# A third of an attention tile's probabilities turned by VectorE and a trip through DRAM instead of TensorE, in a three-layer Perceiver kernel

## The reference, cut to what matters

```python
def attention(q, k, v, mask):          # 32 heads of 32, 8 groups that share keys and values
    scores = einsum('bsgrd,btgd->bgrst', q, k) / sqrt(32) + mask
    probs = softmax(scores)            # over the 257 context rows
    return einsum('bgrst,btgd->bsgrd', probs, v)
x = x + attention(layernorm(x), ctx, ctx, mask)
x = x + state_space(layernorm(x))      # a causal convolution with one kernel of 1024 taps, plus D*u
x = x + experts(layernorm(x))          # 64 rank-8 experts, the top 16 of each row weighted by a softmax
```

## Time and profile before

| | |
|---|---|
| median of 3 runs | 1291.4 us (1287.3 to 1295.49) |
| the profiled execution, its own time | 1286.13 us |
| its span from the first to the last instruction | 1284.3 us |
| busy | TensorE 96%, ScalarE 87%, VectorE 76%, GpSimd 64% |
| mean granted TensorE clock | 0.993 of full speed |

### The profile page before, as it was taken

The page is one execution under the profiler, slowest core; times in us unless marked ns, Lnnn a source line. Parts: engine busy times, 40 slices in busy tenths (PEclk is TensorE's granted clock), DMA queues, the critical chain, the costliest instruction groups (busy, mean ns, idle before and its releaser), DMA issues.

```text
span 1284.3 us, 41514 instructions
## 1 busy us (share of the span) xinstructions
PE 1238.2 (96%) x13676; PEld 1075.3 (84%) x13676; DVE 976.1 (76%) x3424; ACT 1121.2 (87%) x3337; POOL 827.1 (64%) x1259
## 2 busy tenths in 40 slices
PE   4679999999999999999999999999999999999997
PEld 3568888888888888888888888888888888888886
DVE  7877777877777777777877877778777777777753
ACT  6999999999899989898998989999998999899851
POOL 5477667677666667766767766676776666677420
PEclk9799999999999999999999999999999999999999
DMA  7543444444443444444344444444444434444210
GB/s 246 158 148 114 139 120 137 139 130 139 130 139 109 148 138 123 130 146 125 117 139 155 122 122 147 117 133 139 137 138 123 139 118 139 138 124 127 55 60 33
DMA packets 150103, 166.38 MB, mean 130 GB/s; under 512 B 58217, under 2 KB 116082, under 8 KB 149890
## 3 DMA queue, kind: packets, MB, share of 16 engines
q1 hardware_dynamic: 149890, 163.72, 42.7%
HBM read 128.50 MB, written 34.08 MB: 127 GB/s over the span
## 4 chain that ended last, share of the span: by engine, by line
PE 93%; ACT 2%; DVE 2%; DMA 1%; issue 1%; POOL 0%; SPq 0%; DVEq 0%; ACTq 0%; POOLq 0%
PE ps_p L561 27%; PE ps_p L647 17%; PE ps_p L632 17%; PE ps_p L660 14%; PE ps_p L593 10%; PE ps_s L573 9%; ACT pr L851 1%; DMA tmp<-in_wide 0%; ACT pts L783 0%; DMA qx<-turn_q 0%; DVE ms L1398 0%; DVE x L1254 0%; PE ps_p L519 0%; DMA turn_q<-xq 0%; ACT xq L865 0%
## 5 line engine op out<-in xcount | busy, mean ns | idle before, releaser
L851 ACT ACTIVATE pr<-ms,negmax 128x256 f32<-128x256 f32 x1024 | 513.8, 505 | 1.4 <-DVE negmax L1398 1.3
L1398 DVE CUSTOM_DVE_ANT_0 ms<-ps_s,neg_mask,last 128x256 f32<-128x256 f32 x1024 | 455.2, 473 | 55.4 <-PE ps_s L573 55.1
L783 ACT ACTIVATE pts<-ps_p 128x512 f32<-128x512 f32 x512 | 296.4, 593 | 51.4 <-PE ps_p L561 47.5
L561 PE MATMUL ps_p<-ident,pr 128*128 128x128 f32 x2048 | 305.2, 277 | 9.6 <-ACT pr L851 3.5
L561 PEld LDWEIGHTS ps_p<-ident,pr 128*128 128x128 f32 x2048 | 239.2, 141 | 46.1 <-issue 13.7
L851 ACT ACTIVATION_READ_ACCUMULATOR pr<-ms,negmax 128x1 f32 x1024 | 200.4, 196 | 0.0
L1072 POOL TENSOR_TENSOR kt<-kr,kt 128x512 fp32r<-128x512 f32 x128 | 165.6, 1293 | 29.5 <-ACT kt L783 29.5
L647 PE MATMUL ps_p<-wa_hi,ut_hi 128*128 128x288 f32 x512 | 177.6, 347 | 1.4 <-DVE ut_lo L1214 1.4
L647 PE MATMUL ps_p<-wa_lo,ut_hi 128*128 128x288 f32 x512 | 151.2, 295 | 0.0
L647 PE MATMUL ps_p<-wa_hi,ut_lo 128*128 128x288 f32 x512 | 150.6, 294 | 0.0
L1114 POOL TENSOR_TENSOR lastp<-lastp 128x256 f32<-128x256 f32 (+4 forms) x320 | 129.8, 405 | 22.6
(11 more groups left out here) (139 smaller groups left out, 2562.5 us busy)
## 6 DMA issues: line engine op xcount, KB each, us to landing
cx<-in_ctx SPq DMA_DIRECT2D x128, 256.0 KB, 3.1
kr<-in_keys SPq DMA_DIRECT2D x128, 256.0 KB, 3.7
xq<-in_x SPq DMA_DIRECT2D x32, 512.0 KB, 4.0
turn_q<-xq SPq DMA_DIRECT2D x32, 512.0 KB, 3.7
qx<-turn_q SPq DMA_DIRECT2D x128, 128.0 KB, 2.9
xr<-in_x SPq DMA_DIRECT2D x32, 512.0 KB, 4.3
out_x<-tmp SPq DMA_DIRECT2D x32, 512.0 KB, 5.1
dn<-den SPq DMA_DIRECT2D x512, 2.0 KB, 1.8
```

Of the source, the lines that this page charges most:

```text
L561: mm = pe.transpose(into[:, j * P:(j + 1) * P], source, ident[:, :])
L783: return act.activation(out, in_, ACT.Copy, scale=scale)
L851: act.activation(pr[:, b % 2, g, :], ms[:, n % MS, :], ACT.Exp, bias=negmax[:, n % MS:n % MS + 1], scale=-1.0, accum_out=den[:, b, g:g + 1 ...
L1398: dve.tensor_tensor_reduce(ms[:, n % MS, :], ps_s[:, g % GPH, g // GPH * SW:(g // GPH + 1) * SW], neg_mask[:, 0:SW], 1.0, last[:, it % 2, ...
```

## The change

Batch 2 of each tile (`TURNED = (2,)`) no longer goes through TensorE's transposes. Its `exp` writes `pr` in another column order, so that 32x32 block transposes give what is wanted up to a move of whole partitions; VectorE turns each half of the batch in place (`p_turn`, 128x1024); SP stores each half to DRAM (`store_p`, 512 KB each) and loads it back with four DMAs of 32 partitions (`load_p`, 256 KB each) straight to `pts`. `pair_chunk` and `pair_copy` 8 to 11 go, in every tile. `attend` of batch 2 waits for the load and reads `pts` by a view whose 128 columns are four runs of 32. `pr` is given free by halves of a batch now. All five orders and the table of PSUM banks are written anew.

```diff
+TURNED = (2,)
 BANKS = {
-    "pair": (1, 0, 0, 1, 0, 2, 0, 3, 1, 0, 0, 1, 0, 3, 1, 0,),
+    "pair": (1, 0, 0, 1, 0, 2, 0, 3, 2, 1, 0, 2, 0, 3, 1, 0,),
...
+def paired(m):
+    return sum(k // GPH not in TURNED for k in range(m))
+PAIRS = paired(STEPS // 2)
...
+            def store_p(it, k, h):
+                sp.wait_ge(p_turned[k][h], at(it, 1, 1))
+                if at(it, 64, 0) > 0:
+                    sp.wait_ge(p_loaded[k], at(it, 64, 0))
+                sp.dma_start(turn_p[k, :, :, h, :],
+                             pr[:, TURNED[k] % 2, GPH * h:GPH * (h + 1), :]).then_inc(p_stored[k][h], 16)
+            def load_p(it, k):
+                b = TURNED[k]
+                for h in range(HALVES):
+                    sp.wait_ge(p_stored[k][h], at(it, 16, 16))
+                if at(it, 2 * BPT, 2 * b - 2) > 0:
+                    sp.wait_ge(pv_done, at(it, 2 * BPT, 2 * b - 2))
+                own = pts[:, b % 2 * GPH:(b % 2 + 1) * GPH, :]
+                for i in range(GPH):
+                    sp.dma_start(own[SEQ * i:SEQ * (i + 1), :, :],
+                                 turn_p[k, :, i, :, :].rearrange("(r t) h c -> t r (h c)", r=REP)).then_inc(p_loaded[k], 16)
...
             def attend(it, hh):
-                pe.wait_ge(pc_done, at(it, PAIRS, 2 * hh + 2))
+                if b in TURNED:
+                    pe.wait_ge(p_loaded[TURNED.index(b)], at(it, 64, 64))
+                else:
+                    pe.wait_ge(pc_done, at(it, PAIRS, paired(2 * hh + 2)))
+                turned = pts[:, b % 2 * GPH:(b % 2 + 1) * GPH, :].rearrange("p r (h j q s) -> p h j q r s", h=HALVES, j=TBLK, q=GPH)
...
+                                       turned[:, h, j, q, :, :] if b in TURNED else
                                        pts[:, (2 * hh + q // 2) % PTS, (2 * (q % 2) + j) * P:(2 * (q % 2) + j + 1) * P],
...
             def exp(it, n):
-                    if at(it, PAIRS, 4 * (b - 1)) > 0:
-                        act.wait_ge(pt_done, at(it, PAIRS, 4 * (b - 1)))
+                if g % GPH == 0 and at(it, BPT, b - 2) >= 0:
+                    tile, before, h = (it, b - 2, g // GPH) if b >= 2 else (it - 1, b + 2, g // GPH)
+                    if before in TURNED:
+                        act.wait_ge(p_stored[TURNED.index(before)][h], at(tile, 16, 16))
+                    else:
+                        act.wait_ge(pt_done, at(tile, PAIRS, paired(4 * before + 2 * h + 2)))
+                out, masked = pr[:, b % 2, g, :], ms[:, n % MS, :]
+                if b in TURNED:
+                    out = pr[:, b % 2, g // GPH * GPH:(g // GPH + 1) * GPH, :].rearrange("p g c -> p (g c)").rearrange(
+                        "p (i j g t) -> p g j i t", i=GPH, j=TBLK, g=GPH)[:, g % GPH, :, :, :]
+                    masked = masked.rearrange("p (j i t) -> p j i t", j=TBLK, i=GPH)
...
             def pair_copy(it, m):
-                if at(it, 2 * BPT, (m - PTS) // 2 + 1) > 0:
-                    act.wait_ge(pv_done, at(it, 2 * BPT, (m - PTS) // 2 + 1))
+                read = 2 * (m // GPH) - 2 if (m // GPH - 2) % BPT in TURNED else (m - PTS) // 2 + 1
+                if at(it, 2 * BPT, read) > 0:
+                    act.wait_ge(pv_done, at(it, 2 * BPT, read))
...
+            def p_turn(it, k, h):
+                b = TURNED[k]
+                dve.wait_ge(e_done, at(it, STEPS, GROUPS * b + GPH * (h + 1)))
+                half = pr[:, b % 2, GPH * h:GPH * (h + 1), :].rearrange("p g c -> p (g c)")
+                dve.transpose(half, half).then_inc(p_turned[k][h], 1)
```

More of the change, by code:

```diff
@@ L475, in _ @@
[L475 to L479, removed]
+            load_x(0); load_weight(0); load_s4(); load_router(); load_keys(0, 0); load_wide(); load_mask()
@@ L480, in _ @@
+            store_p(0, 0, 1); load_weight(6); turn_last(1); move_den(0, 2); load_keys(2, 0); load_p(0, 0)
+            load_weight(7); load_context(1, 0); load_residual(0); move_den(0, 3); load_keys(2, 1); load_context(1, 1)
+            load_context(1, 3); store_kernel(); load_last(2); store_q(2); load_strip(); load_keys(2, 2)
+            load_keys(2, 3); move_q(2); move_den(1, 0); move_den(1, 1); load_x(3); store_last(2)
             for it in range(HEAD, TAIL):
                 iteration(it, odd=it % 2)
-            load_residual(30); load_context(31, 0); store(28); turn_last(31); load_context(30, 2); move_den(30, 2)
@@ L485, in _ @@
+            load_context(31, 1); load_p(31, 0); load_context(31, 3); store(29); move_den(31, 3); store(30); store(31)
             sp.wait_ge(out_stored, 16 * TILES)
@@ new lines, in _ @@
+            maximum(0, 23); p_turn(0, 0, 0); s4_step(); p_turn(0, 0, 1); maximum(0, 24); maximum(0, 25)
+            weight_low(4, 1); maximum(0, 26); maximum(0, 27); q_turn(1, 1); maximum(0, 28); maximum(0, 29); s4_step()
+            maximum(0, 30); maximum(0, 31); s4_step(); q_stats(2, 0); maximum(1, 0); weight_low(5, 0); maximum(1, 1)
+            q_stats(2, 1); maximum(1, 2); maximum(1, 3); maximum(1, 4); weight_low(5, 1); maximum(1, 5); maximum(1, 6)
+            maximum(1, 7); weight_low(6, 0); q_stats(2, 2); weight_low(6, 1); s4_step(); normalisers(0); s4_step()
@@ new lines, in _ @@
+            maximum(1, 8); s4_step(); maximum(1, 9); maximum(1, 10); maximum(1, 11); maximum(1, 12); maximum(1, 13)
+            maximum(1, 14); maximum(1, 15); out_half(0, 0); weight_low(7, 0); out_half(0, 1); u_stats(0, 0)
+            maximum(1, 16); u_stats(0, 1); u_stats(0, 2); maximum(1, 17); maximum(1, 18); maximum(1, 19)
+            maximum(1, 20); maximum(1, 21); maximum(1, 22); p_turn(1, 0, 0); maximum(1, 23); strip_low(0)
+            strip_low(1); strip_low(2); maximum(1, 24); maximum(1, 25); u_low(0, 0); q_turn(2, 0); p_turn(1, 0, 1)
@@ L1639, in _ @@
+            u_low(0, 1); maximum(1, 26); maximum(1, 27); second_residual(0, 0, 0); maximum(1, 28); maximum(1, 29)
+            maximum(1, 30); weight_low(7, 1); q_stats(3, 0); q_turn(2, 1); maximum(1, 31); second_residual(0, 1, 0)
+            q_stats(3, 1); z_low(0, 0); z_stats(0, 0, 0); z_low(0, 1)
             for it in range(HEAD, TAIL):
                 iteration(it, odd=it % 2)
[L1641 to L1642 removed]
@@ new lines, in _ @@
+            route_step(29, 2); route_step(29, 3); normalisers(30); maximum(31, 8); maximum(31, 9); maximum(31, 10)
+            maximum(31, 11); route_step(29, 4); maximum(31, 12); route_step(29, 5); maximum(31, 13); maximum(31, 14)
+            route_step(29, 6); route_step(29, 7); maximum(31, 15); route_step(29, 8); route_step(29, 9); gated(29, 1)
+            out_half(30, 0); gated(29, 0); out_half(30, 1); u_stats(30, 0); maximum(31, 16); maximum(31, 17)
+            maximum(31, 18); gated_low(29); maximum(31, 19); u_stats(30, 1); maximum(31, 20); u_stats(30, 2)
@@ new lines, in _ @@
+            route_step(30, 2); normalisers(31); route_step(30, 3); route_step(30, 4); route_step(30, 5)
+            route_step(30, 6); route_step(30, 7); out_half(31, 0); route_step(30, 8); route_step(30, 9); gated(30, 1)
+            out_half(31, 1); gated(30, 0); gated_low(30); u_stats(31, 0); u_stats(31, 1); u_stats(31, 2)
+            third_residual(30, 0, 0); u_low(31, 0); u_low(31, 1); second_residual(31, 0, 1); third_residual(30, 1, 0)
+            z_stats(31, 0, 1); second_residual(31, 1, 1); z_stats(31, 1, 1); z_low(31, 0); z_stats(31, 2, 1)
```

509 lines of the change are left out of this document (237 added, 272 removed).

## The result

The changed kernel takes 1408.5 us (1405.0 to 1408.6, four runs) beside 1292.6 (1287.3 to 1295.5, four runs) for the kernel before: a ratio of 1.091, 95% interval 1.088 to 1.094. It is 9.1% slower. The forecast was 1231 us, faster, with a range up to 1258: wrong in sign.

The account below looks back on a forecast made before the run. TensorE alone was taken to bound 85% of the time: 1286.1 - 59.5 (iterations) + 5.8 (slip) - 2 (head) - 1.8 (tail) = 1228.6 us, set at 1231 for the runs' median; range 1215 to 1258.

Parts of the forecast that it names:

- TensorE's list: TensorE's work in an iteration: four chunks and two turns to the whole array fewer, 2.05 us off 37.73, making 35.7.
- the slip of 0.2 us: Allowance on each iteration for three thin margins of 0.15 to 0.3 us: 5.8 us in all, ends 0 and 1 us.
- A: Rival: VectorE becomes the bound in the iterations, 36.8 us each, 1255 us in all; chance 0.16.
- C: Rival: strided reads of `attend` or writes of `exp` cost their upper bound, 1260 us; chance 0.08 together with B in part.
- `p_turn` 1.25 us: VectorE's in-place transpose of 128x1024, taken between 1.13 and 1.40 us; two add 2.5 us to an iteration.
- `attend'4` due at 42.6: TensorE reaches the turned batch's first `attend` 35.7 + 6.9 us after iteration start; turn ends at 28.2, loads land at 39.5.
- SP reaches `load_p` 5.5 us after the turn: SP's list: turn ends at 28.2 us, SP issues context, den, turn_last and keys moves, reaching `load_p` at 33.7.
- Landing 5.8 us after the first issue: Four loads of 256 KB, 2.2 + 4 x 0.9 us, landing at 39.5; upper bound 10.2 us, 43.9.
- rival B: Loads land late at `attend'4`, kernel gets slower, 1327 us at a 3.6 us stall; chance 0.06 in full.
- 3 us more issue, with 5.2 us of air: SP's queue in an iteration: six more issues of 0.5 us, set against the air that one wait alone gives.
- A late landing costs its whole excess: At `attend'4`: a late load stops three engines and costs the full time by which it is late.
- the head's -2 us: Head, ScalarE busiest: loses eight copies, 3.9 us, VectorE gains four turns, 5 us; -2 us, ends -8 and +8.

Follow-up runs that it names:

- first run: Changed kernel without the turned batch's two stores and four loads, their waits becoming waits for the turn (`p_turned`): 1225.3 us.
- third run: Changed kernel with batch 3's four den moves issued right behind the turned batch's loads on SP's list, nothing left out: 1350.0 us.
- ninth: The fifth run with the turned batch's loads sent to a DRAM scratch tensor and `attend` waiting only for the turn: 1317.6 us.
- tenth: SP's order only, beside the fifth run: turned half stored at once, residual and context 1 loads moved to mid-iteration, output store behind the loads: 1405.0 us.
- twelfth: The ninth with runs of 128 bytes in place of 1 and 2 KB, same issues and waits: 1251.5 us.
- thirteenth: The eleventh with the loads sent to a DRAM scratch tensor and `attend` waiting only for the turned half: 1291.8 us.
- fifth run: Changed kernel, SP's order spread: context 2 and residual loads to mid-iteration, output store ahead of turned batch's loads, batch 3's den moves right behind them: 1354.3 us.
- eleventh: Changed kernel with the turned batch's two stores and four loads issued by ScalarE on its own queue instead of SP: 1460.7 us.

## Why the prediction was wrong

By its own steps:

- TensorE's list, 35.7 us an iteration: right, 35.4 without transfers, so the slip of 0.2 us wasn't needed. The rivals A and C fall: VectorE is busy 518.88 of 600 us there, 30.6 of 35.4, with nobody waiting long for it; `exp` takes 502 ns a piece; `attend` of the turned batch takes 1.08 us at the full clock like any other.
- `p_turn` 1.25 us: right, 1.244 (median).
- `attend'4` due at 42.6 with the turn ended at 28.2, 14.4 us apart: right, 14.5 in the first run.
- SP reaches `load_p` 5.5 us after the turn: mis-sized. It took 9.1 (726.2 to 735.2 in the iteration shown). The mean of nine iterations is 8.3. I left out the stores' own issues, which end 0.9 us after the turn, and issues took longer than the earlier trace rows gave: context'2 1.07 us for some 0.5, den'2 4.18 for 2.5, with single moves at up to 1.1 us (median 0.59). turn_last took 1.94, as priced. Why an issue takes longer here wasn't tried.
- Landing 5.8 us after the first issue: mis-sized, 8.1 (mean of nine iterations 8.4). I added lone rows of 256 and 512 KB; but four transfers of the same list share those 8.1 us, and DMA was 0.92 busy. Together 17.2 for 11.3, which overdraws the 14.4. This was rival B, at its place and past its point (5.9 us later than my walk, where it decided from 5.1). I gave it 0.06, against it "busy 0.45 of the time": the mean of an iteration, for a burst that fills the engines. But B isn't the answer either: TensorE waits 2.0 us for the load, and by B's own price that only uses up the gain, 1286.1 + 29 x (2.0 - 2.05) - 4 = 1281 us.
- The step that failed altogether stands nowhere in the sum. I asked what the queue ahead does to the new load and never what the load does to the queue behind: den'3, the output store, residual and contexts. Each landing that they need comes later, `attend'4` to the next turn grows from 20.9 to 24.4 us, and this is more than the 2.3 us by which `attend'4` is later. The third run buys 58 us back by changing nothing but the place of four moves of 2 KB.
- SP "3 us more issue, with 5.2 us of air": the size was right and the reading wrong. Air ahead of one wait doesn't shorten the way between two others. The ninth, tenth and twelfth runs show the path through SP's ordered issues and waits: SP has 21, 27 and 10% of their chains, 1% of the first run's.
- "A late landing costs its whole excess": too little. To the wait comes the lower clock behind it. In the iteration shown, the three products behind a wait of 2.59 us take 1.30, 1.65 and 1.70 us for 1.08, 0.98 and 1.08 at the full clock:

```profile
743.35:747.90 4.55, 4.55 (x89) 3.65 (x90) 0.00 (x0) 1.84 (x5) 0.00 (x0) 0.62 0.59 212
```

- Head and tail: by the first transposes of an iteration, the iterations start at 102.9 us before, 114.0 after and 108.1 without transfers. So the head's -2 us was mis-sized, +5 even without transfers, within the ends of 8 either way. Of the 180 us between the spans of the changed kernel and the first run, 171 are in the 29 iterations, 6 in the head and 3 in the tail. Why the new head is longer is open.

## What to carry to other kernels

A transfer on an ordered queue has two prices: when it lands, and how much later everything behind it lands. Write down, for each small move behind a new large one, who waits for it and how much air it had, before counting what the compute engines save. Judge room for a burst by the DMA share of the few microseconds in which it runs, not by the mean. And test a suspected wait by opening it: the largest wait of a queue (278 us at one line) was worth nothing, a place on a list was worth 58.

## What the runs showed that I had not expected

- The 2 KB moves of den'3 behind 2.25 MB took 6.5 us to land (median, up to 7.9), 1.7 before (up to 3.2) and 3.0 in the first run, without the turned batch's transfers. On GpSimd's queue the same moves still took 5.2: in these runs small transfers were held up by large ones in flight, on their own queue and beside it.
- A second queue didn't shield anyone: the 256 KB loads landed in 7.6 us (median) from ScalarE's queue and 5.1 from SP's, and with the turned batch's transfers gone from SP's queue the den moves there still landed in 3.0 us in the thirteenth run, 2.3 in the first (medians of 400 to 1000 us).
- The same loads landed in 4.2 us when sent to DRAM and 5.1 to 32 partitions of SBUF (ninth and fifth run), 5.7 and 7.6 from ScalarE's queue (thirteenth and eleventh). The Trainium skill ("SBUF — State Buffer", Door 1: The DMA port swizzle) gives 189 GB/s for 1 MiB into partitions 0 to 31, where one of the four loads goes; by that, as an estimate, 1 MB takes 5.5 us if all four go at that rate in turn. The difference between the runs has the sign of the rule, though who waits changed with the destination, so no run singles it out.
- An issue from ScalarE takes time of its stream: 0.54 us for a store of 512 KB, and 2.13 us for three loads with nothing computed behind them, as shown.
